# Turning a normalised state through four PSUM banks, and five up products ahead of the first gate product

## The reference

```python
x = x + tanh(g_xattn[0]) * L0_xattn(layernorm(x), ctx)      # one head, softmax(ex @ eother.T) @ ctx
x = x + tanh(g_ffn[0])   * L0_ffn(layernorm(x))             # ternary linear, exact gelu, ternary linear
x = x + tanh(g_xattn[1]) * L1_xattn(layernorm(x), ctx, ...) # 16 heads
x = x + tanh(g_ffn[1])   * L1_ffn(layernorm(x))             # gate, up, down, all with fp4 blocks of 16

def _ternary_linear(x, w):          # w in {-1, 0, 1} after rounding
    rms = sqrt(sum(x * x, -1)) / sqrt(d)
    return einsum('bsd,fd->bsf', x / (rms + EPS), w_q)

def nvfp4_linear(x, w, s_in):       # x and w quantised per block of 16, then multiplied
    return einsum('bsh,oh->bso', fake_quant_nvfp4(x, s_in), fake_quant_nvfp4(w, s_w))
```

## Time and profile before

| | us |
|---|---|
| median of three timed runs | 1785.82 |
| lowest, highest | 1785.01, 1788.02 |
| the profiled execution, its time | 1785.0 |
| its span from the first to the last instruction | 1782.9 |
| mean granted TensorE clock | 0.908 of full speed |

### The profile page before, as it was taken

One profiled execution on the slowest core, in us unless ns is written; L12 is line 12 of the kernel. 1 busy time (PEld: TensorE's weight loads), 2 busy tenths in 40 slices (PEclk: granted clock), 3 DMA queues, 4 the chain that ended last, 5 costly groups with the idle time before them and its releaser, 6 DMA issues.

```text
span 1782.9 us, 22428 instructions
## 1 busy us (share of the span) xinstructions
PE 1345.8 (75%) x8120; PEld 693.2 (39%) x8120; DVE 1421.2 (80%) x2437; ACT 692.2 (39%) x2105; POOL 244.8 (14%) x197
## 2 busy tenths in 40 slices
PE   5044837799787978698878888797879886988663
PEld 4021314434453436344543345343634353444321
DVE  6989896877887697787787888778877878786696
ACT  2113206442464327342645156422743264425210
POOL 1102300131003200130013100310022001310000
PEclk9556868999899999999999999998999999999888
DMA  9165861041203320233004210322014100420011
GB/s 350 69 237 144 206 156 36 7 86 39 72 1 60 71 59 13 36 64 78 24 7 89 58 50 1 68 63 60 14 41 90 48 25 7 88 60 24 7 30 47
DMA packets 267395, 119.68 MB, mean 67 GB/s; under 512 B 244090, under 2 KB 244602, under 8 KB 265750
## 3 DMA queue, kind: packets, MB, share of 16 engines
q1 hardware_dynamic: 267286, 118.27, 26.8%
HBM read 49.04 MB, written 8.39 MB: 32 GB/s over the span
## 4 chain that ended last, share of the span: by engine, by line
DVE 46%; PE 32%; ACT 8%; issue 6%; DMA 4%; SPq 2%; POOL 0%; DVEq 0%; ACTq 0%
PE bank L1064 24%; PE bank L1151 6%; DVE amax L819 4%; ACT region L529 4%; DVE hid L824 3%; DVE pair L828 3%; DVE stats L680 2%; DVE th L861 2%; DMA hqt<-pair 2%; DVE region L912 2%; DVE region L711 2%; DVE pair L843 2%; DVE sr L794 2%; DVE hid L865 2%; DVE pair L836 1%
## 5 line engine op out<-in xcount | busy, mean ns | idle before, releaser
L1151 PE MATMUL bank<-w_dn,region 128*128 128x512 fp8e4 x1024 | 243.0, 385 | 36.9 <-DMA region<-region 36.9
L1064 PE MATMUL bank<-w_up,xt 128*128 128x512 fp8e4 x1024 | 245.8, 387 | 31.6 <-ACT region L493 17.0
L1064 PE MATMUL bank<-w_gate,xqt 128*128 128x512 bf16 x512 | 148.9, 418 | 125.4 <-DVE th L861 82.3
L502 ACT ACTIVATE th<-bank,half_cg 128x512 f32<-128x512 f32 x128 | 88.0, 688 | 346.7 <-PE bank L1064 346.7
L420 POOL TENSOR_TENSOR region<-g,region 128x512 f16<-128x512 f32 x128 | 180.4, 1414 | 296.8 <-ACT region L493 288.7
L861 DVE SCALAR_TENSOR_TENSOR th<-th,bank 128x512 f32<-128x512 f32 x128 | 87.7, 685 | 132.8 <-ACT th L502 132.8
L529 ACT ACTIVATE region<-bank,nm 128x77 f32<-128x77 f32 x512 | 161.7, 356 | 63.0 <-DVE nm L907 63.0
L490 ACT ACTIVATE g<-bank 128x512 f32<-128x512 f32 x128 | 76.4, 597 | 245.1 <-PE bank L1064 186.2
L1064 PE MATMUL bank<-w_down,hqt 128*128 128x512 bf16 x512 | 130.3, 413 | 53.4 <-DMA hqt<-pair 53.4
L1151 PEld LDWEIGHTS bank<-w_dn,region 128*128 128x128 f16 x1024 | 101.2, 99 | 162.3 <-DMA region<-region 38.4
L1064 PEld LDWEIGHTS bank<-w_up,xt 128*128 128x128 f16 x1024 | 101.2, 100 | 160.9 <-ACT region L493 20.9
(11 more groups left out here) (206 smaller groups left out, 2449.7 us busy)
## 6 DMA issues: line engine op xcount, KB each, us to landing
xin<-in_x SPq DMA_DIRECT2D x16, 512.0 KB, 4.5
out_x<-x SPq DMA_DIRECT2D x16, 512.0 KB, 2.7
region<-in_w_up_t SPq DMA_DIRECT2D x1, 4096.0 KB, 12.9
hid<-in_gate_w SPq DMA_DIRECT2D x4, 1024.0 KB, 5.4
x<-in_gate_w SPq DMA_DIRECT2D x4, 1024.0 KB, 6.7
hid<-in_up_w SPq DMA_DIRECT2D x4, 1024.0 KB, 5.2
x<-in_up_w SPq DMA_DIRECT2D x4, 1024.0 KB, 5.6
hid<-in_down_w SPq DMA_DIRECT2D x4, 1024.0 KB, 5.0
```

Of the source, the lines that this page charges most:

```text
L502: eng.activation(th[:, u % 2, :], bank[4][:, :], ACT.Tanh, scale=half_cg[:, :]).then_inc(sg["th"], 1)
L1064: last = mm(out, lhs, rhs, start=(n == 0), stop=(n == len(pairs) - 1))
L1151: last = mm(bank[2 + t % 2][:, :], ht[i][:, t % 2, f, :], w_dn[:, f, :], start=(f == 0 and i == 0), stop=(f == KF - 1 and i == 1))
```

## The change

The four tiles of stage 2 are transposed in one step (18) into four banks: tiles 0 and 1 into banks 0 and 1, tiles 2 and 3 into banks 4 and 5, which are free once the last exponentials of the running attention (`p3`) have read them. ScalarE's and VectorE's halves of that step follow in step 19, all four tiles in a row. Up products stand at steps 19, 20, 22, 24 and 25 instead of 20, 21 and 22, and products 0 and 1 wait only for the low parts that they need. Products 3 and 4 so leave slots 3 and 4 of phase B on TensorE; ScalarE's order is as it was. GpSimd's `root4` for tiles 2 and 3 moves from ahead of the first subtraction of phase B to behind the second. New waits keep the order: the transposes of tiles 2 and 3 wait for `p3` of the group before, and gate product 0 for the low parts of the next group's state.

```diff
-T2_AT = {NORM2_AT + 1: (0, 1), NORM2_AT + 2: (2, 3)}
-UP_AT = {NORM2_AT + 3: 0, NORM2_AT + 4: 1, NORM2_AT + 5: 2}
+T2_AT = NORM2_AT + 1
+UP_AT = {NORM2_AT + 2: 0, NORM2_AT + 3: 1, NORM2_AT + 5: 2, NORM2_AT + 7: 3, NORM2_AT + 8: 4}
+ROOT4_AFTER = 1
...
+        def state_bank(stage, t):
+
+            return bank[t % 2 + (4 if stage == 2 and t >= 2 else 0)]
...
             def phase_b(g, s4, g1):
-                if s4 is not None:
-                    root4(s4, 1)
                 for s in range(UP_SLOTS):
...
+                    if s4 is not None and s == ROOT4_AFTER:
+                        root4(s4, 1)
...
-                for t in T2_AT.get(n - 1, ()):
-                    x_hi(2, g, t)
+                if n == T2_AT + 1:
+                    for t in range(TILES):
+                        x_hi(2, g, t)
...
-                for t in T2_AT.get(n - 1, ()):
-                    x_lo(2, g, t)
+                if n == T2_AT + 1:
+                    for t in range(TILES):
+                        x_lo(2, g, t)
...
                 want(pe, f"xn{stage}", g, t + 1)
-                if t >= 2:
+                if t >= 2 and stage == 2:
+                    if g:
+                        want(pe, "p3", g - 1)
+                elif t >= 2:
...
-                for t in T2_AT.get(n, ()):
-                    x_t(2, g, t)
+                if n == T2_AT:
+                    for t in range(TILES):
+                        x_t(2, g, t)
...
                 if s < 2:
-                    want(pe, "xl2", g)
+                    want(pe, "xl2", g, s + 1)
                 else:
                     want(pe, "hh", g, s - 1)
+                    if n == 0 and t >= 2:
+                        want(pe, "xl2", g, t + 1)
...
                     if u == 0 and i == 0:
                         want(pe, "p3", g)
+                        if g + 1 < GROUPS:
+                            want(pe, "xl2", g + 1)
```

More of the change, by code:

```diff
@@ L467, in x_hi @@
                 eng.activation(xt[0][:, :, t * P:(t + 1) * P],
-                               bank[t % 2][:, :].rearrange("p (k t) -> p k t", k=KD),
+                               state_bank(stage, t)[:, :].rearrange("p (k t) -> p k t", k=KD),
                                ACT.Copy).then_inc(sg[f"xh{stage}"], 1)
@@ L716, in x_lo @@
                 sl = slice(t * P, (t + 1) * P)
-                eng.tensor_tensor(xt[1][:, :, sl], bank[t % 2][:, :].rearrange("p (k t) -> p k t", k=KD),
+                eng.tensor_tensor(xt[1][:, :, sl], state_bank(stage, t)[:, :].rearrange("p (k t) -> p k t", k=KD),
                                   xt[0][:, :, sl], ALU.subtract).then_inc(sg[f"xl{stage}"], 1)
@@ L1100, in x_t @@
                 for k in range(KD):
-                    last = tr(bank[t % 2][:, k * P:(k + 1) * P], xn[:, t, k * P:(k + 1) * P], ident[:, :])
+                    last = tr(state_bank(stage, t)[:, k * P:(k + 1) * P], xn[:, t, k * P:(k + 1) * P], ident[:, :])
                 last.then_inc(sg[f"tr{stage}"], 1)
```

## The result

The changed kernel is **slower, by 0.3%**: 1794.47 us against 1787.38 us, medians of 15 runs each, a ratio of 1.0031 (95% interval 1.0020 to 1.0043). That is a small loss, but the interval leaves 1 out. The forecast was 1771.5 us, and the time lies outside its range. The profiled execution took 1792.84 us, with a span of 1790.7 (before 1782.9) and a mean granted clock of 0.896 (before 0.908).

A forecast was written before the change was run, and what follows sets the result against it. It took a chain passing between VectorE and TensorE as the bound. Terms -1.2 - 0.83 + 0 + 0.2 = -1.83 us a seam, -12.8 for seven, -14.3 with the opening, gave 1770.7, so 1771.5 us forecast, range 1766 to 1776.

The forecast's parts named there:

- Term 1: Four banks: head transposes, Gelu 0, up 2 and the fourth tile's output product come earlier, -1.2 us a seam.
- Term 2: Late root: GpSimd's subtractions stretch one of the second-half L849 pair on VectorE instead of both, -0.83 us a seam.
- Term 3: The fourth subtraction leaves L838 and stretches one small instruction among L792 to L799 at the same price: 0 a seam.
- Term 4: Ups 3 and 4 ahead of gate 0, gate 1 at low clock: +0.2 us a seam, -0.97 at full clock.
- The opening: Group 0's first phase A: all four banks turned removes VectorE's wait between its L717s, -1.5 us once.
- The signs named at the end: Expected trace marks: L1230, third Gelu, L849 pair 1.8 us, gate 0 and 1 waits, low clock, seams 189.5 us apart.
- part 1: Four banks: transposes of tiles 2 and 3 moved behind those of tiles 0 and 1, L1230 at 915.7 instead of 916.88.
- the first part: What bounds the kernel: a chain between VectorE and TensorE; a microsecond won before 950.3 in the seam is kept.
- Rival 4: Slower: low clock from gate 1 holds beyond 7.1 us, up 5 at 1.2 GHz, +1.4 a seam, 1796 us; chance 0.08.

The follow-up runs named there:

- experiment 1: The changed kernel with ten extra matmuls into bank 6, never read, just ahead of up product 2 in the seven seams: 1773.91 us, ratio 0.9932.
- experiment 8: The kernel before with only up 1 moved ahead of the head transposes: 1818.79 us, ratio 1.0181.
- experiment 5: The changed kernel without early up products, so four banks and late root with up products at steps 20, 21 and 22: 1759.59 us, ratio 0.9852.
- experiment 2: The changed kernel with up 0 and up 1 back at steps 20 and 21, so up 1 behind the head transposes: 1780.57 us, ratio 0.9968.
- experiment 9: The kernel before with the late root and ups 3 and 4 ahead of gate 0, two banks, up 1 behind the head transposes: 1785.75 us, ratio 0.9991.
- experiment 4: The kernel before with the late root alone: 1782.06 us, ratio 0.9978.
- experiment 7: The changed kernel with ten extra matmuls before up 2 and twenty before gate 1: 1767.02 us, ratio 0.9893.
- Experiment 11: Four banks and late root, up products at steps 20 to 22, extra matmuls ahead of gate 0, gate 13 and the last down product: 1770.64 us, ratio 0.9914.
- experiment 12: Four banks and late root, up products at steps 20 to 22, sixteen extra matmuls ahead of the last down product of stage 4: 1746.71 us, ratio 0.9778.

## Why the prediction was wrong

**Its terms were right where the clock was.** Term 1: -1.2 forecast, -1.21 measured (18.15 for 19.36) in four seams; the two instructions of the first quantisation that GpSimd might stretch were stretched (L835 to 1.53, L843 to 1.26), and L936 still waited 0.36 us for TensorE behind them. Term 2: the pair of L849 at 1.82, as forecast. Term 3: the fourth subtraction meets L803 among the small instructions (0.95 for 0.16), the first L868 stands at 30.67 where 30.75 was forecast (32.78 - 2.03). Term 4: gate 0 after 1.94, gate 1 after 6.00 us at a clock of 0.50, in all seven seams; the step to the fourth L868 is 10.63 for 10.15 counted from the first L861, +0.5 for +0.2, and 11.13, +1.0, in the three long seams, where the low level held for 5.5 us from gate 1 on. The opening gave 0.8 us (the second state's chain stands at 329.3 for 330.1) of 1.5. The signs named at the end, from L1230 to the waits at gates 0 and 1, are there; the last, seams 189.5 us apart, is not.

**The step that failed is in part 1.** It moved L1230 to 915.7 with TensorE going "straight into up 0 (912.2) and up 1", took what follows as earlier by 1.2 us, and never asked what TensorE does between L1230 and up 2. It has nothing to do: the merge, the table load and the Gelus take ScalarE until 919.2, up 1 no longer stands there, and the wait of 1.4 us became 3.1. I asked what the clock does at gates 0 and 1 only, and left it out for the wait that the moved up 1 made, so the term for it was nothing. In three seams it costs 2.9 us, from 18.15 to 21.06. Experiments 1 and 8 show it from both sides: filling that wait gives 18 to 21 us back, opening it in the kernel before costs 32, some 12 of them by the later place.

**The second step that failed is in the first part**: "a microsecond won before 950.3 is kept". It rests on the words that behind 965.45 TensorE runs without a gap. It does so only up to gate 13; the trace before has two long waits further on, of 3.79 and 4.28 us, and the clock was low behind the first in five seams of seven and behind the second in all:

```profile
1021.22 1.04 PE L1064 MATMUL bank<-w_gate,xqt 128*128 128x512 bf16 x4 [3.79 <-DVE th L861]
...
1050.14 5.25 PE L1064 MATMUL bank<-w_down,hqt 128*128 128x512 bf16 x16 [4.28 <-DMA hqt<-pair]
```

In the four seams without a low clock at up 2, the first L868 is 2.1 us earlier than before and the last of the group still 1.6 to 2.0 (the first seam more), but the seam is only 0.3 to 0.8 shorter, again but for the first (2.3). The rest goes mostly in the last down product behind its wait of 4.28 us, which is the same wait as before:

```profile
1048.41 6.54 PE L1071 MATMUL bank<-w_down,hqt 128*128 128x512 bf16 x16 [4.28 <-DMA hqt<-pair]
```

In the kernel before the same sixteen matmuls took 5.25 us at 1050.14, with the low clock over 3.4 us of them; now it covers 6. How long the low level lasts behind a wait is not a property of that wait: an identical stretch, moved by two us, got another 1.3 us of it. Seam by seam the lengths differ from those of before by -2.3, -0.8, +3.7, -0.4, +3.7 and -0.3; with -0.8 in the opening and +4.9 from the start of the seventh to the end that is the 7.8 us between the two spans.

**The place of ups 3 and 4** was priced +0.2 a seam, as a matter of gate 1 alone. Experiment 5 against experiment 2 says 21 us for seven seams, 3 each: 0.8 through GpSimd on L803, 1.0 in the step from the first to the fourth L868 (11.2 for 10.2), and the rest behind the fourth, where the clock is low for longer at the late waits. Without the banks (experiment 9) it is some 2 us in all, with the same 0.8 on L803 and nothing in the step. The prediction had the subtraction on a small instruction in term 3, as a price carried over from L838; experiments 4 and 5 show that without the early up products it falls on nothing ahead of the first L861 or L868, so this 0.8 belongs to them. The rest of their price depends on where in time they fall; the sum could not have found it from one seam.

**The parts are far from equal.** By the ratios: banks -17 us, root -9 on top of them (-4 alone), ups 3 and 4 early +21, up 1 ahead +11 on top (+32 alone): together the +6 of the change, and the whole with the clock held up in two places (experiment 7) is -19. Rival 4, the slower one, forecast 1796 with a chance of 0.08 and so has nearly the measured time, but by the wrong place: it looked for a low clock from gate 1 on that holds beyond 7.1 us, and there it held for 4.5 to 5.5.

**The advice on idle gaps.** I cited the Trainium skill, TensorE: Matmul & The Clock Gate, section Why this matters for your kernels, for the wait before gate 1 only. Its advice, no long idle gaps between bursts, holds for the one before up 2 as well: the trace shows a fall behind 3.09 us in three seams of seven, and before the change none behind 1.4 there, nor behind the 3.3 to 3.5 us ahead of gate 1 in six seams. The same page of the Trainium skill, section What's actually happening, says that the gate runs free and is not reset when a kernel starts; that fits seams which are alike to 0.01 us up to the wait and then differ. Experiment 11 is the limit of the advice: filling gaps, one of them off the path, made the kernel slower.

**What stays open** is why the 3.1 us wait lowers the clock in the seams at 711, 1097 and 1482 and not in the four others. That it depends on absolute time is what the rows suggest, and the one short run of experiment 2 fits it; no run here set that time by itself. Nor is it settled why the clock's share of ups 3 and 4 is large in experiment 5 and small in experiment 9. The late waits were not filled in the changed kernel itself; that they take what is won ahead is read from its rows and from experiments 5 and 12.

## What to carry to other kernels

Moving a product into an idle stretch takes it out of another: list TensorE's waits before and after the change, all of them along the path, and look at each that grows beyond what kept its clock so far. An idle stretch with slow products behind it can be harmless if the clock is back by the time the path needs it; judge it by the first product that somebody waits for. A product that comes earlier also brings forward what follows on other engines: look at what GpSimd's instructions then fall on. Where a wait on the path cannot be shortened, matmuls into a spare bank are a cheap test of the clock's share and can be the fix (1746.7 for 1759.6); in the kernel before, at two late waits, they gained 0.1%, and off the path they did harm.

## What the hardware showed that I had not expected

A wait of 3.1 us, the same in seven seams, was followed by a granted clock of 0.50 in three and of 1.00 in four. The low level behind one and the same wait lasted 3.4 us in one kernel and over 6 in the other. Extra matmuls at one place changed the low stretches at others more than 80 us later: with the ten of experiment 1 the low stretch of 3.4 us that began 114 us after the first seam's start is gone. One kernel took 1779.0 to 1782.3 us in eleven runs and 1767.8 in the twelfth, at a higher mean clock. GpSimd and VectorE stretch each other both ways when they fall together: two subtractions beside the quantisation took 3.62 us (one at 940.92, with no stretched VectorE row beside it, 1.16), and VectorE's L803 took 0.95 where it takes 0.16.
